# Attention and matrix product on one core: the value bias is multiplied through Wo once and added with the output bias, and both heads' contexts are split in one instruction

## The reference, cut to what matters

```python
lv = (hidden_states @ Wlv + blv).reshape(Bq, Sq, NH, D).transpose(0, 2, 1, 3)
...
pl = jax.nn.softmax(sl, axis=-1)
ctx_local = jnp.einsum('bhcqk,bhckd->bhcqd', pl, vw).reshape(Bq, NH, Sq, D)
merged = (ctx_sparse + ctx_local) * 0.5
out = merged.transpose(0, 2, 1, 3).reshape(Bq, Sq, NH * D) @ Wo + bo
```

## Time and profile before

| | |
|---|---|
| runs of the kernel | 2492.33, 2492.66, 2492.68 us; median 2492.66 |
| span of the profiled execution, first to last instruction | 2492.2 us |
| busy share of the span | PE 99%, PEld 88%, DVE 80%, ACT 67%, POOL 70% |
| start of the main loop (step 0) | 37.0 us |
| start of step 255 | 2454.0 us |

### The profile page before, as it was taken

How to read it: one execution, slowest core, us unless ns; L and a number is a source line. 1 busy time by engine, 2 the same in 40 slices (tenths; PEclk the granted TensorE clock), 3 DMA queues, 4 the chain that set the end, 5 groups by cost and what they waited for, 6 DMA issues and landing times. The chain is left out here.

```text
span 2492.2 us, 56206 instructions
## 1 busy us (share of the span) xinstructions
PE 2462.4 (99%) x15574; PEld 2190.6 (88%) x15606; DVE 1996.7 (80%) x6637; ACT 1675.3 (67%) x4866; POOL 1749.7 (70%) x3150
## 2 busy tenths in 40 slices
PE   7999999999999999999999999999999999999998
PEld 6888888888888988888888889888888888888887
DVE  7788888888778887787777888887878878888786
ACT  5667777767666677667666666767676666666665
POOL 6787787776786666666677766666667767676674
PEclk9999999999999999999999999999999999999999
DMA  5433233333332122121441221221235213212301
GB/s 159 136 107 113 71 109 115 117 109 117 123 119 82 52 90 90 60 90 43 151 150 53 81 82 60 90 86 64 78 124 166 94 59 100 75 61 94 98 10 52
DMA packets 183530, 232.36 MB, mean 93 GB/s; under 512 B 19762, under 2 KB 101172, under 8 KB 183220
## 3 DMA queue, kind: packets, MB, share of 16 engines
q1 hardware_dynamic: 182644, 228.50, 28.3%
q10 hardware_dynamic: 576, 0.26, 0.1%
HBM read 162.64 MB, written 65.01 MB: 91 GB/s over the span
## 5 line engine op out<-in xcount | busy, mean ns | idle before, releaser
L1598 POOL TENSOR_TENSOR t<-raw,tB 128x128 f32<-128x128 f32 x512 | 226.4, 464 | 593.8 <-DVE raw L1167 593.7
L987 ACT ACTIVATE ch<-bVC,blT 128x128 fp32r<-128x128 f32 x512 | 160.5, 365 | 511.1 <-PE bVC L726 511.1
L631 PE MATMUL bQK<-wh,xh 128*128 128x512 f32 x1024 | 424.4, 414 | 0.0
L632 PE MATMUL bQK<-wl,xh 128*128 128x512 f32 x1024 | 403.8, 394 | 0.0
L633 PE MATMUL bQK<-wh,xl 128*128 128x512 f32 x1024 | 401.4, 392 | 0.0
L1542 POOL TENSOR_TENSOR r<-ss,mh 128x4 f32<-128x4 f32 x256 | 286.4, 1119 | 60.1 <-DVE ss L1175 57.5
L647 PE MATMUL bVC<-wh,xh 128*128 128x256 f32 x1024 | 310.0, 303 | 0.0
L954 ACT ACTIVATE P<-P,nm,r 128x256 f32<-128x256 f32 (+1 forms) x512 | 295.3, 583 | 0.0
L1203 DVE CUSTOM_DVE_ANT_0 P<-bS,cst 128x256 f32<-128x256 f32 (+1 forms) x512 | 204.2, 399 | 110.5 <-PE bS L679 106.1
L649 PE MATMUL bVC<-wh,xl 128*128 128x256 f32 x1024 | 289.4, 283 | 0.0
L648 PE MATMUL bVC<-wl,xh 128*128 128x256 f32 x1024 | 289.0, 282 | 0.0
(11 more groups left out here) (188 smaller groups left out, 7617.9 us busy)
## 6 DMA issues: line engine op xcount, KB each, us to landing
wh<-kept SPq DMA_DIRECT2D x144, 256.0 KB, 4.1
wl<-kept SPq DMA_DIRECT2D x144, 256.0 KB, 4.6
kept<-wh SPq DMA_DIRECT2D x48, 256.0 KB, 3.2
kept<-wl SPq DMA_DIRECT2D x48, 256.0 KB, 3.4
woh<-kepto SPq DMA_DIRECT2D x48, 256.0 KB, 3.2
wol<-kepto SPq DMA_DIRECT2D x48, 256.0 KB, 3.7
ini<-in_hidden_states SPq DMA_DIRECT2D x24, 256.0 KB, 4.5
xs<-xsh SPq DMA_DIRECT2D x24, 256.0 KB, 2.5
```

The costliest lines, as they stand in the source:

```text
L631: e.matmul(bQK[:, :], a, b, start=kt == 0, stop=False)
L632: e.matmul(bQK[:, :], a, bl, start=False, stop=False)
L1598: last = e.tensor_tensor(t2[:, :, :, d_], raw[:, u % 2, :, :, s_], tB[:, :, u % 8, d_].unsqueeze(1).broadcast_to([128, 2, 2, 32]), ALU.mult)
```

## The change

The bias is no longer added to the contexts. `hi_c` and `lo_c` become one instruction each, over 256 columns, without bias. Instead, `bob` is turned into a table: at the end of VectorE's step 0 it is multiplied by the first column of the identity, which leaves bo in partition 0 and zeros below. Then, each time `lo_wo` splits a chunk of Wo, a new instruction `bias_rows` ahead of it adds to `bob` the raw chunk times the head's column of the bias (16 times in batch 0). In step 62, a new matmul `const_rows` multiplies a matrix of -1 by `bob` into bank bY, which sums over the partitions, and `put_rows` on ScalarE writes its negative back to `bob`; `add_bo` waits for that.

```diff
@@ run_tensor (bias_of is gone from build)
+            def const_rows():
+                e.wait_ge(S["bl"], 2 + 2 * NG)
+                e.wait_ge(S[free["Y"][0]], free["Y"][1])
+                e.matmul(bY[:, :], minus1[:, :], bob[:, :], start=True, stop=True).then_inc(S["bw"], 1)
+                free["Y"] = ("bb", 1)
...
@@ run_tensor, step s, behind both scores(u2, h)
+                if s == 62:
+                    const_rows()
...
@@ run_scalar
                 e.wait_ge(S["c"], 2 * u + 2)
                 if u >= 2:
                     e.wait_ge(S["wo"], u - 1)
-                if u == 0:
-                    e.wait_ge(S["bl"], 1)
-                for h in range(2):
-                    last = e.activation(ch[:, u % 2, h, :], bVC[:, 256 + h * 128:384 + h * 128], ACT.Identity,
-                                        bias=bias_of(u, h))
-                last.then_inc(S["hi_c"], 1)
+                e.activation(pair(ch[:, u % 2]), bVC[:, 256:512], ACT.Copy).then_inc(S["hi_c"], 1)
+
+            def put_rows():
+                e.wait_ge(S["bw"], 1)
+                e.activation(bob[:, :], bY[:, :], ACT.Copy, scale=-1.0).then_inc(S["bb"], 1)
...
@@ run_scalar, step s, ahead of hi_c(u4)
+                if s == 62:
+                    put_rows()
...
@@ run_vector
             def lo_c(u):
                 e.wait_ge(S["hi_c"], u + 1)
-                for h in range(2):
-                    last = e.scalar_tensor_tensor(out=cl[:, u % 2, h, :], in0=bVC[:, 256 + h * 128:384 + h * 128],
-                                                  scalar=bias_of(u, h), in1=f32(ch[:, u % 2, h, :]), op0=ALU.add,
-                                                  op1=ALU.subtract)
-                last.then_inc(S["lo_c"], 1)
+                e.tensor_tensor(pair(cl[:, u % 2]), bVC[:, 256:512], f32(pair(ch[:, u % 2])), ALU.subtract).then_inc(S["lo_c"], 1)
...
+            def bias_rows(q):
+
+                n = o_index(*CHUNKS[q][1:3])
+                e.wait_ge(S["d_w%d" % (q % 2)], 16 * LANDED[q])
+                e.wait_ge(S["bl"], 2 + n)
+                e.scalar_tensor_tensor(out=bob[:, :], in0=wr[:, q % 2, :], scalar=blT[:, n:n + 1], in1=bob[:, :], op0=ALU.mult,
+                                       op1=ALU.add).then_inc(S["bl"], 1)
...
@@ run_vector, step s, behind neg_max(u2)
                 for q, c in enumerate(CHUNKS):
                     if c[0] == "o" and c[3] == s - 1 and c[1]:
+                        bias_rows(q)
                         lo_wo(q)
...
@@ run_vector, end of step 0
                     e.wait_ge(S["d_3"], 32)
                     e.tensor_scalar(blT[:, :], blT[:, :], 0.5, None, ALU.mult, ALU.bypass).then_inc(S["bl"], 1)
+                    e.tensor_scalar(bob[:, :], bob[:, :], ident[:, 0:1], None, ALU.mult, ALU.bypass).then_inc(S["bl"], 1)
...
@@ run_gpsimd, add_bo
                 if t < 8:
                     e.wait_ge(S["acc"], 56 + t + 1)
-                    e.wait_ge(S["d_3"], 32)
+                    e.wait_ge(S["bb"], 1)
```

More of the change, by code:

```diff
@@ L323, in entries_of @@
             return (bY if t < 8 else bT)[:, 0:128]
-        def bias_of(u, h):
-            n = 2 * (u // 8 % NG) + h
-            return blT[:, n:n + 1]
         def both(u, C):
```

## The result

The changed kernel takes 2501.85 us (median of 5 runs, 2501.15 to 2502.79) where the kernel before takes 2492.68: a ratio of 1.0035 with a 95% interval of 1.0023 to 1.0048. The forecast was 2501.0, in a range of 2497.0 to 2504.5, with slower as the likely outcome.

A forecast was written before the change was run, and what follows sets the result against it. The prediction took TensorE, busy 99% of the span, to bound the kernel. Rows +9.4, reduction +0.9 and give-back -1.9 us made +8.4 us, so 2501.0 us, in a range of 2497.0 to 2504.5.

The forecast's parts named there:

- Relief wins: Rival: relief of VectorE and ScalarE adds up along their chain and bias_rows hides, 2486.3 us; chance 0.03.
- (c): bias_rows, 0.67 us each, ahead of wol in batch 0 delay TensorE in eight steps: 9.4 us in sum.
- The two rows hide: Rival: bias_rows ahead of wol cost TensorE nothing, 2491.7 us; chance 0.11, including cases where half hides.
- (e): The plain f32 matmul const_rows is all on TensorE, +0.9 us; put_rows on ScalarE is hidden.
- (f): The merged hi_c and lo_c give back TensorE waits in several steps and at the run's end: -1.9 us.
- the end of the run: Give-back where the ch pair stands ahead of a TensorE wait: 0.25 us, and 0.1 at the last unit.
- the late starts: Give-back of the merged pairs for late starts elsewhere in batch 0: 0.3 us.
- (d): Scaling bob at the end of step 0, some 0.6 us beside TensorE's filler matmuls: costs nothing.
- The ports: Rival: fourteen rows in seven steps each lose 0.2 us or more to GpSimd's shared ports, 2503.9 us; chance 0.08.

The follow-up runs named there:

- experiment 2: Kernel before with only hi_c and lo_c merged into one instruction each, value bias left out altogether: 2490.26 us, ratio 0.9988.
- experiment 1: Changed kernel with the sixteen bias_rows moved to the end of VectorE's step, behind lo_p: 2491.47 us, ratio 0.9994.
- experiment 3: Changed kernel with both bias_rows right behind both wol in seven steps, still ahead of lo_x; step 5 as changed: 2495.0 us, ratio 1.0006.
- experiment 5: Changed kernel with the two-instruction forms of hi_c and lo_c put back, so the bias is in the output twice: 2506.66 us, ratio 1.005.
- experiment 4: Changed kernel without const_rows and put_rows; add_bo adds the table as it stands: 2500.75 us, ratio 1.003.
- experiment 9: Changed kernel with a second, zero-column instruction behind the first half's row only, three rows ahead of the last wol: 2512.51 us, ratio 1.0076.
- experiment 6: Changed kernel with each of the sixteen bias_rows followed by a second of the same size with a zero column: 2522.87 us, ratio 1.0118.
- experiment 11: Kernel before with GpSimd's split of the next weights waiting for nm in two of its steps: 2492.11 us, ratio 0.9992.

## Why the prediction was right

**What bounds the kernel.** That relief of VectorE and ScalarE is worth only what TensorE waits for them held: the pairs made one take 47.6 us off VectorE's busy time and 62.4 off ScalarE's, and gave 2.6 us. *Relief wins* (2486.3) was excluded by experiment 2, which has the relief and nothing else and is at 2490.26.

**(c), the rows.** Predicted 9.4 us, measured 9.14: 5 (0.67, measured 0.88), 13 (1.2, 1.04), 21 (1.34, 1.33), 29 (1.15, 1.16), 37 (1.2, 1.20), 45 (1.34, 1.31), 53 (1.15, 1.15) and 61 (1.34, 1.07). The 0.67 us a row was right, and so were the places of the waits, L737 at 0.14 us behind `wol` and L652 behind `lo_x`. Experiments 1 and 3 show that the rows' place makes the cost, and not their work. Three sizes were off. I had step 61 repeat step 21. But VectorE reaches `wol` there 0.27 us earlier once either part of the change is in: 4.15 us into the step before, 3.87 with the merge alone, and 3.87 and 3.88 for the first row in experiment 5 and in the changed kernel, as in step 37. So TensorE waits 0.97 us as in step 37 (0.96), and not 1.46. Why VectorE is earlier there stays open. In step 13 the merge alone gives 0.38 (experiment 2), which I had put at nothing; the rows cost 1.42 against it, more than the 1.2 of the sum, as the second took 0.96 us. In step 5 a row took 0.96 us instead of 0.75, which is 0.2 of the 0.21 missed. *The two rows hide* is excluded by each of the eight steps. All of the loss lies in batch 0, as forecast: the start of step 64 moved by 8.1 us, and what follows is 1.3 us shorter, a little more than the 1 us that I had allowed.

**(e), the reduction.** Predicted 0.9, measured 0.86 by experiment 4.

**(f), the give-back.** Predicted 1.9, measured 2.57. The mechanism was right: steps 23, 47, 104, 168, 76 and 140 gave 0.15 to 0.25 each. The terms that were short are step 17 (0.39 for 0.19, nearly the savings of both engines together, 0.25 + 0.19), the end of the run (0.53 for 0.35), the late starts (0.40 in steps 12 and 28 for 0.3) and four steps at 0.23 to 0.24 for 0.19.

**(d), the scaling of `bob`.** It took 1.54 us, where I had put some 0.6, and still cost nothing that shows in a step.

**The sum.** The steps give 9.14 + 0.86 - 2.57 = +7.4 us where I had +8.4. The median came out 9.2 above that of before, within 0.8 us of the forecast but on its other side. That is luck in part: the steps say 1.0 us less than the sum, the medians 0.8 more, and what all makes up the 1.8 us between steps and medians is not shown. The start of the run differs by 0.6 us in the two profiled executions, and the one of before was not a typical one: its span plus what the other executions had on top, 1.8 to 2.2 us, is 1.3 to 1.7 above its median.

**The ports.** For this kernel the rival was wrong: of the fourteen rows in the seven steps one, the second of step 13, took 0.96 us, and the others 0.74 to 0.77. It and the second row of step 5, 0.96 us as well, ran while GpSimd was at work. So did the first rows of both steps, at 0.75 and 0.77, but in the six steps from 21 on GpSimd was idle, as the prediction had it. So these runs don't refute the price as such: the late rows of experiment 1, all beside GpSimd, took 0.77 to 1.02 us.

**What the prediction lacked.** That a wait of TensorE can cost more than its own length. The changed kernel's waits, up to 1.77 us, stayed just on the good side in its profiled execution; one of the same length did not in experiment 5. With three rows instead of two ahead of the last `wol` (experiment 9) a forecast by length alone would have been 5 us short, for a reason that is in none of the terms.

## What to carry to other kernels

Before an instruction is put on an engine that has room, ask who waits for what stands behind it in the same list: sixteen instructions of 0.75 us cost 9 us ahead of `wol` and, in the best places found, 0.4 us behind it. Behind means behind every such wait, and also with its buffers released no later, for SP's queue passes the delay on to loads that have nothing to do with it. If TensorE must wait, look at its clock in the stretch that follows; the slower matmuls there cost another 1.4 to 1.8 us here, and once 3.1.

## What the runs showed of the hardware

- **The clock behind a wait.** TensorE's waits of 0.96 to 1.77 us in the changed kernel were followed by the full clock, 2.4 GHz, in its profiled execution. Behind waits of 2.87 to 3.65 us (experiment 6, five steps) it ran at 1.2 GHz for part of the step; 1.4 to 1.7 us more than the two rows' length was lost each time, and 3.1 us behind the longest. Between, it went either way: full after 1.75 us (experiment 9, steps 37 and 61), 1.96 us (experiment 3, steps 29 and 53), 1.99 and 2.56 us (experiment 9, steps 13 and 29) and 2.54 us (experiment 6, step 37), half after 1.76 us (experiment 5, step 53), 2.38, 2.47 and 2.56 us (experiment 9) and 2.54 us (experiment 6, step 61). The half clock began between 1.4 us ahead of the end of the wait (experiment 6, step 45) and 1.8 us behind it (experiment 5). What decides between equal waits stays open.
- **A small instruction under a long one.** `nm`, on 4 columns, takes 0.16 us alone and 1.24 beside GpSimd's subtraction, and two such cases cost the kernel before 0.95 us each. One wait of GpSimd for `nm`, in two steps, gives 1.9 us by steps (experiment 11).
- **A plain f32 matmul** of 512 columns with an f32 weight has two records and holds TensorE for 0.86 us, where one fp32r product of 512 columns holds it for 0.23.
